# A block-wise FP4 quantization on one engine, split over three and pipelined by one tile

## What is computed

```python
xb = x.reshape(shape[:-1] + (shape[-1] // 16, 16))
scale = max(max|xb| / 6, 1e-12)
idx = searchsorted([.25, .75, 1.25, 1.75, 2.5, 3.5, 5.], |xb / scale|)
q = [0, .5, 1, 1.5, 2, 3, 4, 6][idx] * sign(xb / scale) * scale
...
h = silu(q(xn) @ q(w_gate).T) * (q(xn) @ q(w_up).T)
ffn = q(h) @ q(w_down).T
```

## Time and profile before

| | |
|---|---|
| three runs | 5535.71, 5541.3, 5544.7 us (median 5541.3) |
| profiled execution | 5516.46 us, span of its slowest core 5514.9 us |
| spans of the eight cores | 5505.6 to 5514.9 us |
| DVE busy | 3864.8 us, 70% |
| PE busy | 2104.0 us, 38% |
| ACT busy | 682.8 us, 12% |
| POOL busy | 185.3 us, 3%, all of it DMA issues and five memsets |
| stages on that core | A 92 to 500 and 872 to 1268, W 1636 to 2960, D 2960 to 5515 us |

### The profile page before, as it was taken

How to read it: one execution, slowest core, us unless ns; L and a number is a source line. 1 busy time by engine, 2 the same in 40 slices (tenths; PEclk the granted TensorE clock), 3 DMA queues, 4 the chain that set the end, 5 groups by cost and what they waited for, 6 DMA issues and landing times. The chain is left out here.

```text
span 5514.9 us, 38460 instructions; the slowest of 8 cores (5505.6 to 5514.9 us)
## 1 busy us (share of the span) xinstructions
PE 2104.0 (38%) x12373; PEld 1037.7 (19%) x12373; DVE 3864.8 (70%) x4521; ACT 682.8 (12%) x1430; POOL 185.3 (3%) x249
## 2 busy tenths in 40 slices
PE   1665465664460000000003354354345434533543
PEld 0222432223330000000001121122112112211221
DVE  3885327882339999999997766776676667667766
ACT  0222211222200000000001010011011101100110
POOL 0001110001100000000000000000000000000000
PEclk9776567775575555555556677677677767776776
DMA  4221132111140000000000000000000000000000
GB/s 77 69 69 54 47 93 99 61 62 56 47 140 27 27 27 27 27 27 25 24 29 15 10 19 19 19 10 19 19 10 19 19 19 10 19 19 19 10 19 17
DMA packets 86045, 196.60 MB, mean 36 GB/s; under 512 B 42295, under 2 KB 42311, under 8 KB 85847
## 3 DMA queue, kind: packets, MB, share of 16 engines
q0 software_dynamic: 26544, 100.74, 5.9%
q1 hardware_dynamic: 59304, 93.42, 5.7%
HBM read 135.41 MB, written 67.12 MB: 37 GB/s over the span
## 5 line engine op out<-in xcount | busy, mean ns | idle before, releaser
L65 DVE SCALAR_TENSOR_TENSOR sc<-sc 128x1024 f32<-128x1024 f32 (+1 forms) x588 | 688.4, 1171 | 63.4 <-DVE sc L62 1.8
L69 DVE SCALAR_TENSOR_TENSOR sc<-sc 128x1024 f32<-128x1024 f32 (+1 forms) x588 | 688.4, 1171 | 63.1 <-DVE sc L69 1.4
L824 PE MATMUL psT<-ident,wq_bf 128*128 128x128 bf16 x528 | 67.1, 306 | 1263.9 <-DVE wq_bf L78 1263.9
L1012 DVE TENSOR_TENSOR sc<-pairbuf 128x512 f32<-128x512 f32 x96 | 65.9, 686 | 608.0 <-ACT pairbuf L991 608.0
L967 PE MATMUL psA<-wdqT,hqT 128*128 128x512 bf16 x1408 | 378.9, 438 | 37.6 <-ACT hqT L997 36.4
L941 PE MATMUL psQ<-wgqT,sexp 128*128 128x512 bf16 x384 | 117.4, 461 | 618.0 <-DMA sc<-partial_dram 588.2
L941 PE MATMUL psQ<-wgqT,attn_tm 128*128 128x512 bf16 x384 | 116.4, 458 | 613.1 <-DMA sc<-partial_dram 570.1
L989 ACT ACTIVATE pairbuf<-psQ 128x512 f32<-128x512 f32 x96 | 57.3, 597 | 2149.7 <-PE psB L941 1937.8
L824 PEld LDWEIGHTS psT<-ident,wq_bf 128*128 128x128 bf16 x528 | 50.9, 138 | 1280.0 <-issue 1280.0
L76 DVE TENSOR_TENSOR sc<-sc 128x1024 f32<-128x1024 f32 (+1 forms) x196 | 229.4, 1170 | 21.4 <-DVE sc L74 1.4
L71 DVE SCALAR_TENSOR_TENSOR sc<-sc 128x1024 f32<-128x1024 f32 (+1 forms) x196 | 229.4, 1171 | 20.8 <-DVE sc L69 0.5
(11 more groups left out here) (163 smaller groups left out, 4307.8 us busy)
## 6 DMA issues: line engine op xcount, KB each, us to landing
sc<-xin SPq DMA_DIRECT2D x64, 512.0 KB
qkv_dram<-qkv_tile POOLq DMA_DIRECT2D x32, 768.0 KB, 3.6
partial_dram<-sc POOLq DMA_DIRECT2D x32, 512.0 KB, 3.4
sc<-partial_dram SPq DMA_DIRECT2D x32, 512.0 KB
out<-sc POOLq DMA_DIRECT2D x32, 512.0 KB, 2.9
wrow<-wg SPq DMA_DIRECT2D x22, 512.0 KB
wrow<-wu SPq DMA_DIRECT2D x22, 512.0 KB
xqT_dram<-xqTst POOLq DMA_DIRECT2D x32, 256.0 KB, 4.4
```

Source lines behind the costliest of these rows:

```text
L65: sv.inc(vec.scalar_tensor_tensor(L[:, 0:n], a2[:, 0:n], c, L[:, 0:n], ALU.is_gt, ALU.add))
L69: sv.inc(vec.scalar_tensor_tensor(S[:, 0:n], a2[:, 0:n], c, S[:, 0:n], ALU.is_gt, ALU.add))
L824: m = tensor.transpose(psT[:, 128 * k:128 * (k + 1)], wqW[c % 2][:, 128 * k:128 * (k + 1)], ident[:])
```

## The change

The quantization is cut in two. `_q_pre` keeps the block maximum, the scales and the product with 1/scale on DVE. ACT then makes the square (Square) and the sign (Sign); POOL makes the counts of the three high midpoints (tab for two of them, tc for twice the third); `_q_post` on DVE counts the low midpoints and combines.

```diff
+def _q_scal(scal, v_ap, a2_ap, sgn_ap, ss):
+    ss.inc(scal.activation(a2_ap, v_ap, AF.Square))
+    ss.inc(scal.activation(sgn_ap, v_ap, AF.Sign))
+def _q_pool(g, a2_ap, n, tab, tc, sq):
+    sq.inc(g.tensor_single_scalar(tc[:, 0:n], a2_ap, TSQ[0], ALU.is_gt))
+    sq.inc(g.tensor_single_scalar(tab[:, 0:n], a2_ap, TSQ[1], ALU.is_gt))
+    g.wait_ge(sq.h, sq.v)
+    sq.inc(g.tensor_tensor(tab[:, 0:n], tab[:, 0:n], tc[:, 0:n], ALU.add))
+    g.wait_ge(sq.h, sq.v)
+    sq.inc(g.tensor_scalar(tc[:, 0:n], a2_ap, TSQ[2], 2.0, op0=ALU.is_gt, op1=ALU.mult))
+    g.wait_ge(sq.h, sq.v)
+def _q_post(vec, nblk, bstats, boff, a2, sgn, tab, tc, L, out_bf, sv):
...
+    sv.inc(vec.tensor_single_scalar(L[:, 0:n], a2[:, 0:n], TL[0], ALU.is_gt))
+    for c in TL[1:]:
+        vec.wait_ge(sv.h, sv.v)
+        sv.inc(vec.scalar_tensor_tensor(L[:, 0:n], a2[:, 0:n], c, L[:, 0:n], ALU.is_gt, ALU.add))
...
+    sv.inc(vec.scalar_tensor_tensor(L[:, 0:n], tab[:, 0:n], 2.0, L[:, 0:n], ALU.mult, ALU.add))
...
+    sv.inc(vec.scalar_tensor_tensor(L[:, 0:n], tc[:, 0:n], 2.0, L[:, 0:n], ALU.mult, ALU.add))
...
+    sv.inc(vec.tensor_mul(L[:, 0:n], L[:, 0:n], sgn[:, 0:n]))
...
+    sv.inc(vec.tensor_tensor(seg(out_bf), seg(L[:, 0:n]), bc(hsc), ALU.mult))
```

DVE runs `_q_post` of a tile (chunk, pair) after `_q_pre` of the next. The v, a2 and tab buffers are doubled; the sign buffer and tc (but for W's tc) are single. ACT in A, for tile t:

```diff
 Sqrt(t); eviction of xn(t-1); six QKV evictions of t-1
+if t <= T - 1:
+    scal.wait_ge(sv.h, EVA[("v", t)])
...
+    ss.inc(scal.activation(a2Ab[t % 2][:], vAb[t % 2][:], AF.Square))
 eviction of the quantized t-1
+    if t >= 1:
+        scal.wait_ge(sv.h, EVA[("q1", t - 1)])
+    ss.inc(scal.activation(sgnA[:], vAb[t % 2][:], AF.Sign))
```

POOL makes its four instructions of tile t ahead of the stores of tile t-1. In W, ACT waits for "v" of chunk c and for "q1" (the sign product, the last pass but one of `_q_post`) of chunk c-1 ahead of both Square and Sign, and evicts chunk c-1 behind them. In D the two copies of the up halves are gone, and DVE reads them from PSUM:

```diff
-ss.inc(scal.copy(pb2[:, 1024:1024 + iwA], psU[:, 0:iwA]))
-ss.inc(scal.copy(pb2[:, 1536:1536 + iwB], psB[:, 512:512 + iwB]))
+scal.wait_ge(sv.h, EVD[("v", gt, pq)])
...
+ss.inc(scal.activation(a2Db[Pg % 2][:, 0:pw], vDb[Pg % 2][:, 0:pw], AF.Square))
+if pv is not None:
+    scal.wait_ge(sv.h, EVD[("q1",) + pv])
+ss.inc(scal.activation(sgnD[:, 0:pw], vDb[Pg % 2][:, 0:pw], AF.Sign))
...
-sv.inc(vec.tensor_mul(sc2[:, 0:iwA], pb2[:, 0:iwA], pb2[:, 1024:1024 + iwA]))
+sv.inc(vec.tensor_mul(sc2[:, 0:iwA], pb2[:, 0:iwA], psU[:, 0:iwA]))
...
+gpsimd.wait_ge(ss.h, EVD[("a2", gt, pq)])
+if pv is not None:
+    gpsimd.wait_ge(sv.h, EVD[("comb2",) + pv])
+_q_pool(gpsimd, a2Db[Pg % 2][:, 0:pw], pw, tabD[Pg % 2], tcD, sq)
```

More of the change, by code:

```diff
@@ L29 @@
 QUANT_INCS = 19
+QPRE_INCS = 5
+QPOST_INCS = 8
+QSC_INCS = 2
+QPL_INCS = 4
 class Sem:
@@ new lines, in build_nc, with prevp @@
+            pwidths = [1024, 1024, 768]
+            def prevp(gt, pq):
+                P = 3 * gt + pq - 1
+                return (P // 3, P % 3) if P >= 0 else None
+            EVD = {}
+            cs, cv, cp, cq = ssD, svD, stnD, sqD
+            for gt in range(NTOT + 1):
+                if gt <= NTOT - 1:
+                    for pq in range(3):
+                        cp += 1
+                        EVD[("pair", gt, pq)] = cp
+                if gt >= 1:
+                    for g in range(3):
+                        cp += 1
+                        EVD[("tg", gt - 1, g)] = cp
+                    cp += 1
+                    EVD[("down", gt - 1)] = cp
+                if gt <= NTOT - 1:
+                    for pq in range(3):
+                        cs += 1; EVD[("siluA", gt, pq)] = cs
+                        cs += 1; EVD[("siluB", gt, pq)] = cs
+                        cs += 1; EVD[("a2", gt, pq)] = cs
+                        cs += 1; EVD[("sgn", gt, pq)] = cs
+                if gt >= 1:
+                    for g in range(3):
+                        cs += 1; EVD[("evac", gt - 1, g)] = cs
+                if gt <= NTOT - 1:
+                    for pq in range(3):
+                        cv += 1; EVD[("hmA", gt, pq)] = cv
+                        cv += 1; EVD[("hmB", gt, pq)] = cv
+                        cv += QPRE_INCS; EVD[("v", gt, pq)] = cv
+                        pv = prevp(gt, pq)
+                        if pv is not None:
+                            cv += QPOST_INCS
+                            EVD[("post",) + pv] = cv
+                            EVD[("L3",) + pv] = cv - 4
+                            EVD[("comb2",) + pv] = cv - 2
+                            EVD[("q1",) + pv] = cv - 1
+                elif NP >= 1:
+                    pv = (NTOT - 1, 2)
+                    cv += QPOST_INCS
+                    EVD[("post",) + pv] = cv
+                    EVD[("L3",) + pv] = cv - 4
+                    EVD[("comb2",) + pv] = cv - 2
+                    EVD[("q1",) + pv] = cv - 1
+                if gt >= 1:
+                    cv += 2
+                    EVD[("adds", gt - 1)] = cv
+                if gt <= NTOT - 1:
+                    for pq in range(3):
+                        cq += QPL_INCS
+                        EVD[("pool", gt, pq)] = cq
@@ L910, in _ @@
                                 sync.wait_ge(sp.h, spD + gt - 1)
-                                sync.wait_ge(stn.h, pairv(gt - 2, 2))
+                                sync.wait_ge(stn.h, EVD[("pair", gt - 2, 2)])
                             sync.dma_start(
@@ L971, in _ @@
                                 stn.inc(m)
-                                assert stn.v == down_done(gt - 1)
+                                assert stn.v == EVD[("down", gt - 1)]
                     @blk.scalar
@@ L1020, in _ @@
+                                    _q_pre(vec, sc2[:, 0:pw], pw // 16, bstats,
+                                           88 * (Pg % 2), vDb[Pg % 2], sv)
+                                    assert sv.v == EVD[("v", gt, pq)]
+                                    pv = prevp(gt, pq)
+                                    if pv is not None:
+                                        emit_post(pv)
+                            elif NP >= 1:
+                                emit_post((NTOT - 1, 2))
                             if gt >= 1:
-                                vec.wait_ge(stn.h, down_done(gt - 1))
+                                vec.wait_ge(stn.h, EVD[("down", gt - 1)])
```

468 lines of the change are left out of this document (304 added, 164 removed).

## The result

The kernel after the change took 6619.9 us (median of 10 runs, 6573.6 to 6674.4); the kernel before, on the same chips, 5531.9 (10 runs, 5513.0 to 5548.6). The ratio is 1.194 [1.191, 1.198]: 19% slower. The direction was as forecast (5843 us), the size was not, and the time lies outside the range of 5640 to 6120. In some executions of either kernel the cores of one die run at a lower granted clock and take up to some per cent longer; the ratios leave these out. The profiled execution took 6564.1 us, its slowest core 6562.6; that is 1047.7 us more than the span before.

A forecast was written before the change was run, and what follows sets the result against it. DVE was taken to bound W directly, A until the PE-ACT ring binds, and D only outside 20.5 us a tile. The terms -215 + 346 + 80 + 75 + 16 = +302 on 5541.3 gave 5843 us, range 5640 to 6120.

The forecast's parts named there:

- R: GpSimd's time for its four new instructions per quantization, taken as 6.5 us, bounded by 3.3 and 9.8.
- signs of being wrong: The forecast is wrong if A's QKV isn't serial with `_q_post`, R is under 4 or over 9, or passes stretch.
- W: -215: Stage W (weights, 68 chunks): ring of Square, GpSimd and `_q_post` takes 10.0 + R = 16.5 us a chunk, saving 215.
- A: +346: Stage A (norm, quantization, QKV; 32 tiles): a new ring through ACT's queue takes 35.3 us a tile instead of 23.8.
- D: +80: Stage D (FFN, 32 tiles): 82.3 us a tile instead of 79.8, with 17 us of DVE work gone, 19 of waiting added.
- The slip of the down projection: Stage D: hqT evictions queue behind the third pair's Sign, so DVE waits 17 to 19 us before the adds.
- enters from 7.1: Stage D: R matters only from 7.1 us, GpSimd having 7 to 8 us from the last read of tcD.
- Sharing: +75 and +16: One-input DVE passes wait for the GpSimd instruction in flight: +75 us in A, +16 in D, none in W.
- GpSimd slow: Rival: R = 9.8 makes W 0 instead of -215, A +75, D +150, giving 6280 us; chance 0.07.
- Exclusive passes: Rival: two-input DVE passes exclude GpSimd too, adding 95 us in W and 130 in D, giving 6068; chance 0.23.
- Table switches: Rival: Square or Sign need another ACT table, 2.6 us a tile in A and D, giving 6003; chance 0.05.
- The down projection early: Rival: no slip in D, 63 us a tile, 5230 in all; chance 0.06, shared with a shorter ring in A.

The follow-up runs named there:

- Experiments 2: Changed kernel with ScalarE's Square moved ahead of the six QKV evictions in stage A: 6391.4 us, ratio 1.153.
- 3: Changed kernel with Square, Sign and the next tile's Sqrt all ahead of the QKV evictions in stage A: 6129.1 us, ratio 1.109.
- experiment 1: Changed kernel with GpSimd's four instructions cut to 16 columns, all waits and queue orders kept: 5489.4 us, ratio 0.988.
- 5: Changed kernel with a second sign buffer in stage W, so Square and Sign wait for the chunk two before: 6292.2 us, ratio 1.135.
- 6: Kernel before, plus four unused GpSimd compares beside each chunk of stage W: 5769.4 us, ratio 1.044.
- 4: Changed kernel with the three hqT evictions ahead of the third pair's Sign in stage D: 6274.6 us in the profiled run, 6310.9 in a second.
- experiment 8: Changed kernel with all three repairs together (3, 4 and 5): 5462.1 us, ratio 0.989.
- 9: As experiment 8, but DVE counts the high midpoints again and GpSimd does no elementwise work: 4978.1 us, ratio 0.903.
- experiment 7: Kernel before, plus four unused GpSimd memsets beside each chunk of stage W: 5576.0 us, ratio 1.007.

## Why the prediction was off in size

The step that failed is one term: **R**, "I take 6.5 us", with "upper bound: every one as two 1.23 passes, 9.8 us". It measured 11.9 us from the first instruction's start to the start of `_q_post` in W, 12.2 in A and 13.7 in D. Two of the prediction's own signs of being wrong came true with it, R over 9 and stretched passes. Both bounds were made of DVE's rates, and GpSimd has its own: a compare over 1024 columns 2.77 us (4 times DVE's 0.69), with a multiplication in the same instruction 3.63, the addition 2.12 (1.7 times DVE's 1.23). I had also guessed that an addition costs two passes and a compare one; the compare is the dearer one. The Trainium skill's figure for the addition ("GPSIMD Engine Reference", Performance versus the Vector engine), which the prediction halved to 2.25, was near the 2.12.

The same steps with the measured R:

| | formula of the prediction | with 6.5 | with R of the trace | measured |
|---|---|---|---|---|
| W | 10.0 + R | 16.5 | 21.9 | 21.95 |
| A | 35.3, + 1 per us above 7.5 | 35.3 | 40.0 | 39.8 (mean), 40.4 (the tile shown) |
| D | 82.3, + waits for GpSimd | 82.3 | 82.3 + 5.94 + 3.67 = 91.9 | 92.4 |

- **W: -215** became +147 (2.2 us in each of 60 full chunks is 132, the rest lies in the narrow ones and at the stage's ends). The ring was right; with R = 11.9 it is dearer than the DVE queue of 19.75 that it replaces.
- **A: +346** became +507 (16.0 x 30 steps is 479, the rest lies in the loops' first and last steps). Experiments 2, 3 and 1 show its parts: 16.7 us of ACT's order, of which 5.7 are R behind the evictions. The bare ring measured 34.1 against 35.3; the largest part of that is transposes, QKV and evictions, 15.6 us where I had 16.6 (from the end of `_q_post` to the Square).
- **D: +80** became +394. The slip of the down projection was there (16.5 us of wait, a bare ring of 80.9 against 82.3) and priced a little too high: the prediction added 2.0 us to a down product of 12.6 for the lower clock level, and in the tile shown the adds start 11.6 us after its first matmul. R "enters from 7.1", and at 13.7 it enters at two of three boundaries with 9.6 us, 308 in 32 tiles.
- **Sharing: +75 and +16.** The stretching was there, and one-input passes are held by GpSimd as assumed: apply 1.49 instead of 0.81 in A, small scalings up to 2.07 instead of 0.20. But with R at 12 DVE waits for GpSimd behind these passes anyway, so they cost nothing in A. What sharing costs is what it adds to R itself: nothing in W (11.3 and hand-overs), 0.3 in A, and 1.8 in D, where the two-input passes hold up GpSimd's instructions; in D some 1.9 us a tile come on top that neither the bare ring nor the waits for GpSimd hold (92.4 - 80.9 - 9.6). The prediction had priced that effect only as a rival.
- **Rivals.** *GpSimd slow* had the right mechanism, and R = 9.8 with 6280 us came nearest; it had 0.07. *Exclusive passes* (0.23) is right in one direction: a two-input pass holds a reading GpSimd instruction off until it ends (1). The other way round such a pass is delayed by up to 1.7 us and they still overlap (5, 6). What sets the length of that delay is left open. *Table switches* did not occur: the trace of the kernel after has six table loads in all, as that before. *The down projection early* took 10.2 us from a tile, not the 19 of its price, in part because of GpSimd.

What is shown: GpSimd's elementwise time costs some 1,130 us (1 against after). By the lengths of the stages in the profiled runs, ACT's order costs 508 us in A (3), Sign ahead of the evictions 318 in D (4), the single sign buffer 296 in W (5). The last three lie in different stages and add up: together they are 1,122, and experiment 8 gives 1,080. The first is another cut through the same loss and isn't added to them. Taking GpSimd's elementwise work out on top of the three repairs gives 484 more (9).

## What to carry to other kernels

When an idle engine is to take over work, price it by rows of that very engine, operation and width; where there is none, let the upper bound be several times the other engine's rate, and see from which value on the ring that it closes is longer than the queue it relieves (here 9.8 us in W). A piece that is pipelined by a tile has to be placed ahead of the older work in every queue it passes: three instructions behind six evictions cost 17 us a tile here. And first look for passes the bound engine need not do: three fewer DVE instructions a quantization and two adds moved gave 16%, with no work for anyone else.

## What the runs showed of the hardware that was not expected

- GpSimd, 128 x 1024 elements, alone: compare with a scalar 2.77 us, compare and multiply 3.63, addition of two bf16 or f32 tiles 2.12, memset 0.95; at 16 columns 0.22 to 0.28. The Trainium skill ("GPSIMD Engine Reference", Engine selection) calls one-input elementwise work roughly as fast as on VectorE; here it was four times slower than the 0.69 of DVE, and slower than the two-input addition.
- A DVE pass with two inputs in SBUF holds off a GpSimd instruction that reads until the pass has ended: 1.28 us instead of 0.24 for 16 columns, in all 95 cases beside one line of DVE (experiment 1). The other way round such a pass is delayed, 1.23 to 1.87 or 2.96, but not for the whole GpSimd instruction; full-width compares on GpSimd go from 2.77 to between 2.8 and 3.9.
- A one-input f32 pass of DVE is mostly held until the GpSimd instruction in flight has ended, also when that only writes: in experiment 7, 54 of 67 of the small scalings L53 end 0.05 us after a memset.
- DVE multiplies with one input in PSUM took 0.69 us for 512 columns, as with both in SBUF; the two ACT copies that the change removed had saved DVE nothing.
